# Own scores ahead of the preceding unit's transposed scores on TensorE, in attention slots without an expert tile

## What is computed

```python
B, S, SE, D, H, FF, E, K = (2, 256, 256, 128, 16, 512, 8, 2)
HD = D // H
...
x = _layernorm(x + _attn(x, x, x, sa_..., True), ln1_g, ln1_b)
x = _layernorm(x + _attn(x, encoder_output, encoder_output, ca_..., False), ln2_g, ln2_b)
x = _layernorm(x + _moe(x, router_w, router_b, e_w1, e_b1, e_w2, e_b2), ln3_g, ln3_b)
# _attn
scores = jnp.einsum('bhqk,bkhd->...', Q, Kp) / sqrt(HD);  a = softmax(scores);  o = a @ V @ wo + bo
# _moe
topw, topi = top_k(softmax(x @ rw + rb), 2);  h = gelu(x @ w1 + b1);  out = sum of topw * (h @ w2 + b2)
```

## Time and profile before

| what | value |
|---|---|
| time, median of 3 runs | 773.73 us (770.77 to 774.32) |
| span of the profiled execution | 818.8 us |
| TensorE busy | 601.7 us (73%) |
| VectorE busy | 489.2 us (60%) |
| ScalarE busy | 439.9 us (54%) |
| GpSimd busy | 369.8 us (45%) |

### The profile page before, as it was taken

One profiled execution on the slowest core, in us unless ns is written; L12 is line 12 of the kernel. 1 busy time (PEld: TensorE's weight loads), 2 busy tenths in 40 slices (PEclk: granted clock), 3 DMA queues, 4 the chain that ended last, 5 costly groups with the idle time before them and its releaser, 6 DMA issues. The chain is left out here.

```text
span 818.8 us, 21239 instructions
## 1 busy us (share of the span) xinstructions
PE 601.7 (73%) x7870; PEld 476.9 (58%) x7870; DVE 489.2 (60%) x1337; ACT 439.9 (54%) x814; POOL 369.8 (45%) x576
## 2 busy tenths in 40 slices
PE   2689687657667898877798776777767778588780
PEld 1356455445445676765676565667656667478570
DVE  4488998769987777786676677342465420402134
ACT  1246455335434599976797676555744454244120
POOL 7133443424348344427653572771654752600620
PEclk9989977879968899998998999799888789799886
DMA  4463445663224564544554454665544468588421
GB/s 111 113 207 95 140 131 171 203 194 105 59 82 133 167 177 143 171 142 136 158 167 130 124 155 137 199 197 167 157 127 149 135 214 260 163 266 261 147 62 32
DMA packets 141413, 124.64 MB, mean 152 GB/s; under 512 B 12224, under 2 KB 123600, under 8 KB 141312
## 3 DMA queue, kind: packets, MB, share of 16 engines
q1 hardware_dynamic: 134496, 113.06, 45.8%
q0 software_dynamic: 4368, 9.05, 3.8%
q10 hardware_dynamic: 2448, 1.18, 0.5%
HBM read 86.81 MB, written 38.54 MB: 153 GB/s over the span
## 5 line engine op out<-in xcount | busy, mean ns | idle before, releaser
L1727 PE MATMUL bank<-w_in,w_hl 128*128 128x128 f32 x704 | 109.2, 302 | 1.5 <-issue 1.3
L1172 DVE TENSOR_REDUCE row_max<-bank 128x16 bf16<-128x1024 f32 x64 | 78.2, 1223 | 49.0 <-PE bank L1589 48.2
L1727 PEld LDWEIGHTS bank<-w_in,w_hl 128*128 128x128 f32 x704 | 95.8, 210 | 1.9 <-issue 1.4
L966 ACT ACTIVATE probT<-bank 128x1024 f32<-128x1024 f32 x64 | 65.5, 1023 | 56.8 <-PE bank L1613 39.7
L836 POOL TENSOR_TENSOR veps<-mv,eps 128x1 f32<-128x1 f32 x64 | 15.7, 246 | 170.6 <-DVE mv L1210 170.6
L850 POOL TENSOR_TENSOR prob_lo<-probT,prob_hi 128x384 f16<-128x384 f32 x64 | 67.7, 1057 | 51.2 <-ACT prob_hi L969 50.7
L1713 PE MATMUL bank<-xT,w_in 128*128 128x128 f16 x1056 | 81.4, 231 | 2.9 <-issue 2.9
L1018 ACT ACTIVATE w_hl<-bank 128x512 f32<-128x512 f32 x88 | 52.5, 597 | 55.6 <-PE bank L1713 35.8
L875 POOL DMA_INDIRECT w_hl<-ys,pos x52 | 52.0, 999 | 49.9 <-DMA ys<-w_hl 34.8
L1713 PEld LDWEIGHTS bank<-xT,w_in 128*128 128x128 f16 x1056 | 69.6, 104 | 3.9 <-issue 3.8
L859 POOL DMA_INDIRECT xs<-x_hl,pos x60 | 62.8, 1047 | 17.7 <-issue 17.7
(11 more groups left out here) (182 smaller groups left out, 1581.0 us busy)
## 6 DMA issues: line engine op xcount, KB each, us to landing
w_in<-w_scr SPq DMA_DIRECT2D x96, 512.0 KB
q_scr<-q_hl SPq DMA_DIRECT2D x64, 128.0 KB
k_scr<-k_hl SPq DMA_DIRECT2D x64, 128.0 KB
q_st<-q_scr SPq DMA_DIRECT2D x32, 256.0 KB, 2.9
k_all<-k_scr SPq DMA_DIRECT2D x128, 64.0 KB, 2.2
xs_tile<-xs SPq DMA_DIRECT2D x42, 128.0 KB
ys<-w_hl SPq DMA_DIRECT2D x42, 128.0 KB
xs<-xs_tile SPq DMA_DIRECT2D x3, 1472.0 KB, 6.9
```

The source lines that it names most:

```text
L966: act.activation(probT[u.buf][:, :, :].rearrange("p h q -> p (h q)"), bank[:, KEYS:KEYS + 2, :].rearrange("p a n -> p (a n)"), ACT.Exp, sc ...
L1172: dve.reduce_max(row_max[u.buf][:, :], bank[:, SC:SC + 2, :].rearrange("p a (h k) -> p (a h) k", k=S), AX.X).then_inc(max_done[a], 1)
L1727: last = pe.matmul(expert_y(x), hid[x.par][:, c, :], w2_t[x.wb][:, c, :], start=False, stop=c == FC - 1, skip_group_check=True)
```

## The change

In slots in which `turns_late` holds, TensorE's list has the slot's own scores ahead of the transposed scores of the unit before; in the others the order stays. Nothing else changes: the instructions are the same ones, each with its own waits, and the lists of the other engines stay as they are.

```diff
@@ -1783,9 +1783,11 @@
                     turn_both(g)
                 if (c := chunk_closes(g)) is not None:
                     down(Tile(FIRST_TILE[c] + TILES_OF[c] - 1))
+                if turns_late(g) and (u := unit_at(g)):
+                    scores(g, u)
                 if u := unit_at(g - 1):
                     scores_T(g, u)
-                if u := unit_at(g):
+                if not turns_late(g) and (u := unit_at(g)):
                     scores(g, u)
                 if turns_late(g):
                     turn_both(g)
```

## The result

| | median | range, runs | against the kernel before, 95% interval |
|---|---|---|---|
| before | 773.73 us | 770.77 to 776.34, 5 | |
| changed | 781.65 us | 778.42 to 785.84, 5 | 1.0118 (1.0080 to 1.0157) |
| changed, measured again later | 777.20 us | 775.01 to 781.20, 6 | 1.0083 (1.0053 to 1.0113), before at 771.22 |

The forecast was 779.5 us (+0.75%). A cost in us is the ratio times the time of before. Weighted by their intervals, the two ratios of the changed kernel give +0.96% with a half width of 0.24, or 7.4 us.

A forecast was written before the change was run, and what follows sets the result against it. VectorE was taken to bound most touched slots, DMA arrivals slots 12 to 21. Terms 0 - 1.1 + 2.4 + 0 + 2.2 + 0.5 + 2.4 = +6.4 us, scaled +6.0, forecast 779.5 us; range 770 to 787, the forecast's own 777.5 to 782.5.

The forecast's parts named there:

- the landing slots: Slots 14, 18, 20, 22, waiting on DMA: transposed scores and exponentials move behind the wait; +2.4, 0, +2.2, +0.5 us.
- the shift is carried to the end: From slot 33 on the order is unchanged and slots hang together, so the profile's +6.4 us persists, scaled to +6.0.
- Early slots: Slots 1 to 5 gain, VectorE about 3 us ahead in slot 4, but 0 by slot 9; bounds -3 and +1.
- the transposed scores cannot slip past waiting scores: TensorE keeps matmuls in program order, so ready transposed scores stay behind waiting scores; otherwise the DMA terms would be 0.
- Where TensorE doesn't wait for `max_diag`: Scores delay the chain to the logits: slots 15 and 16 +1.0, 23 to 25 +0.4, 32 +1.0; total +2.4 us.
- slots 12 and 13: Turning of tokens comes about a scores' time earlier there: -1.1 us.
- TensorE's slack: TensorE's 20.9 us of waiting for `max_diag` in 17 places, read as slack in half the slots.
- No change: Losses are swallowed as in slot 18, VectorE's work filling slots 22 to 27: about +1 us, 775; chance 0.22.
- faster: Early 3 us kept, scores hide in `max_diag` waits, DMA waits short without a profile: -4.5 us scaled, 769; chance 0.14.
- Much slower: Chain of scores, transposed scores, exponentials, copy and logits sets the pace of slots 14 to 32: +12 us, 785; chance 0.10.
- Doesn't do what it says: TensorE reaches scores no earlier, its prior work ending after `max_diag`; only half the losses: +4 us, 777.5; chance 0.12.

The follow-up runs named there:

- the kernel with the turnings ahead: Changed kernel with both turnings between own scores and transposed scores, ScalarE's copies of turned tiles ahead of the exponentials: 773.79 us, 1.0039 against the kernel before.
- the second profile of before: Unchanged kernel run again against itself, no edit, giving another profile with a span of 771.8 us: 773.31 us, 1.0026.
- the run with all slots but the four: Kernel before, given the new order in all touched slots except 14, 18, 20 and 22: 774.24 us, 1.0041.
- the run with both remedies: Changed kernel with slots 14, 18, 20 and 22 in the old order, turnings and their copies ahead in other touched slots: 772.68 us, 0.9996 against the kernel before.

## Why the prediction was right, by its own steps

**Sign and size: right; the mechanism: right for the landing slots, and only in part borne out for the rest.** The forecast's +6.4 us in the profile at slot 33 compares with 7.3 us (mean of two profiles each, which scatter by up to 3.7), its +0.75% with +0.96% (0.72 to 1.20). The working has two slips that change nothing: 773.73 + 6.0 is 779.7 and not 779.5, and the first group of 1.03 us that I put in slot 20 is that of slot 21 (in the changed kernel slot 20's took 1.03 too). The step that the shift is carried to the end holds only roughly, as the kernel with the turnings ahead shows.

**Early slots, 0 (bounds -3 and +1): right.** The run of slots 0 to 9 measured +0.07%. The gain to slot 4, about 3 us, is there, and S2.0 and S3.0 stand for their landings (2.01 and 2.45 us in the changed kernel, where both profiles of before had no such wait). Slot 8 works as worked out: its VectorE instructions wait for ScalarE's conversions of the expert weights (changed kernel):

```profile
81.17 0.74 ACT L1064 ACTIVATE b_hi<-b_in 8x640 f16<-8x640 f32 x1
81.93 0.63 ACT L1065 ACTIVATE w_hl<-w_in 128x512 f16<-128x512 f32 x1
81.94 0.81 DVE L1430 SCALAR_TENSOR_TENSOR b_all<-b_in,b_hi 8x640 f16<-8x640 f32 x1 [1.88 <-ACT b_hi L1064]
...
82.78 0.69 DVE L1437 SCALAR_TENSOR_TENSOR w_hl<-w_in,w_hl 128x512 f16<-128x512 f32 x1
```

VectorE waits 1.88 us for them at L1430, in the two profiles of before not at all and 0.74. The conversions themselves are not later than before: L1065 starts at 81.93, and at 79.21 and 83.07 there. The row maxima of slot 9 stand at 92.94, against 90.97 and 94.45. The early microseconds had turned into waiting by then.

**The landing slots, +5.1 in all (2.4, 0, 2.2, 0.5): right in sum, 4.7 us measured (2.7 to 6.8).** The closeness to 5.1 is partly luck, since the split isn't confirmed. Slots 14 and 18 gave 2.5 of it (0.2 to 4.9) where 2.4 and 0 were worked out. Slots 20 and 22 alone gave 0.2 instead of 2.7, with an interval from -2.3 to +2.8. Whether they cost only together with 14 and 18 is open. That slot 18's loss is taken back in slot 20 fits the wait there, which shrank from 6.03 and 6.06 us to 4.40 and 3.82 in the two profiles of the changed kernel. In the changed kernel the local times were in the range given: 4.83 behind the scores in slot 18 (3.7 to 4.9), logits 4.28 behind in slot 20 (4.1 to 4.9; 185.60 less 181.32).

I said that by the rule of the Trainium skill, "TensorE: Matmul & The Clock Gate", section "Step-by-step: what each phase is for", the transposed scores cannot slip past waiting scores. The trace agrees: in slot 18 they start at 160.74, directly behind scores that had waited 6.19 us.

**Where TensorE doesn't wait for `max_diag`, +2.4, and slots 12 and 13, -1.1: the mis-sized term.** Together +1.3; the run with all slots but the four measured 3.2 us (1.1 to 5.2), and putting the copies ahead of the exponentials gave 3.4 us back. The best value is thus some 3 us, more than twice the term, though 1.3 lies just inside the interval; that the chain over exponentials and copies is what costs them fits both runs but is argued, not shown, as said above. The places weren't confirmed: slots 15 and 16, 23 to 25 and 32 cost nothing measurable when they are changed in their own group. Yet in the whole the profiles lose more there than forecast: from the row maxima of slot 21 to those of slot 26 the changed kernel takes 40.77 and 38.97 us, the kernel before 37.03 and 36.57, where slots 22 to 25 were given +0.9. With slots 23 to 32 alone it is 36.64, so what slots 22 to 25 lose depends on the slots ahead of them, and why stays open. What I had counted as TensorE's slack, 20.9 us ahead of `max_diag`, is used up (0.9 us left), and TensorE's waits for ScalarE's copies ahead of logits and projection are 21 us longer than in the second profile of before.

**The rivals.** "No change" and "faster" are outside both intervals of the whole. "Much slower" named the chain through the logits, which is where the waits grew, but its price isn't right: +12 us was forecast for it, some 3 measured. "Doesn't do what it says" falls with the wait for `max_diag`.

## What to carry to other kernels

On an engine that takes its work in order, an instruction that waits for a transfer should have as little ready work behind it as possible: here four of 33 exchanges alone cost 0.61% where all together cost 0.96%. An exchange on one engine is to be followed through every other engine's list: the copies for the logits stood behind exponentials that had become later, and moving them ahead brought 0.44 points back, of which a part may be a gain of its own. An idle time that is removed is worth something only if what it held up was what ends last: in the run with both remedies the row maxima waited 9.8 us for scores instead of 17.7 and 21.1, and no gain was measured.

## What the runs showed of the chip that I had not expected

The stretch from the row maxima of slot 71 to the end, in which all these kernels do the same work in the same order but for slot 71 itself, took between 180.0 and 185.4 us, and the granted clock from 660 to 680 us goes with it at its extremes. The unchanged kernel (180.0 us), the changed one (184.9) and the one with the turnings ahead (185.4), in the columns of the earlier trace rows:

```profile
660.00:680.00 20.00, 15.54 (x199) 14.66 (x197) 3.01 (x12) 8.76 (x24) 9.51 (x11) 1.00 0.92 294
```

```profile
660.00:680.00 20.00, 15.69 (x172) 14.76 (x171) 0.00 (x0) 7.17 (x20) 4.16 (x5) 0.83 0.72 223
```

```profile
660.00:680.00 20.00, 16.17 (x171) 15.65 (x170) 4.88 (x18) 7.36 (x18) 11.67 (x14) 0.78 0.82 269
```

Of 13 profiles (the first of the unchanged kernel left aside, with 214.4 us), the four at a clock of 1.00 there took 180.0 to 182.3 us, the one at 0.96 took 182.4, the five at 0.91 181.5 to 185.2, and the three at 0.78 or 0.83 184.1 to 185.4. The kernel with the turnings ahead reached slot 71 5.9 us before the second profile of the unchanged one and ended 0.5 us before it. The window was picked after the fact, and the one ahead of it doesn't show the same: from 640 to 660 us the changed kernel has 1.00 like the unchanged one, and the one with the turnings ahead 0.96. Whether the clock makes the work late or the other way round isn't settled either; but 4.9 of the 11.3 us between the spans 771.8 and 783.1 arise in this stretch, and a single pair of profiles would have blamed them on the change.
